# Four graph layers on one core: the normalised adjacency and the masks prepared in layer 0's second step, and the first two aggregations run between layer 0's last products

## The reference

```
x = layernorm(x + L0(x, adj))      # h = x W^T + b, then 8 Euler steps:
                                   #   h += dt * (alpha/2 * (adj h - h) + h w_eff - h + x)
x = layernorm(x + L1(x, adj))      # A = adj + I; deg = row sums + column sums - diagonal
                                   # A_hat = A * deg^-1/2[:, None] * deg^-1/2[None, :]
                                   # agg = A_hat x; h = relu(batchnorm(agg W1^T + b1)); out = batchnorm(h W2^T + b2)
x = layernorm(x + L2(x, adj))      # attention with 4 heads, masked where adj == 0
x = layernorm(x + L3(x, adj))      # graph attention with leaky relu, masked where adj == 0
```

## Time and profile before

| | us |
|---|---|
| median of 3 runs | 969.47 (965.02 to 971.21) |
| span of the profiled execution | 965.1 |
| busy: TensorE, weight load, VectorE, ScalarE, GpSimd | 905.8, 646.9, 641.5, 508.7, 382.7 |

### The profile page before, as it was taken

One profiled execution on the slowest core, in us unless ns is written; L12 is line 12 of the kernel. 1 busy time (PEld: TensorE's weight loads), 2 busy tenths in 40 slices (PEclk: granted clock), 3 DMA queues, 4 the chain that ended last, 5 costly groups with the idle time before them and its releaser, 6 DMA issues. The chain is left out here.

```text
span 965.1 us, 20989 instructions
## 1 busy us (share of the span) xinstructions
PE 905.8 (94%) x6054; PEld 646.9 (67%) x6054; DVE 641.5 (66%) x1944; ACT 508.7 (53%) x919; POOL 382.7 (40%) x433
## 2 busy tenths in 40 slices
PE   6999999999999699977789999999999998999996
PEld 5799999999999688833345544555445453677775
DVE  4754554554554576646466777777777764899997
ACT  4323121121121245555356777777777767788884
POOL 4011121021020130000246777878778777355554
PEclk9999999999999899979889999999999999999999
DMA  8000000000000100000033334333333342011111
GB/s 245 23 12 12 12 23 12 12 22 11 11 11 0 30 15 0 0 1 0 1 79 77 78 71 87 72 79 85 66 81 83 66 87 46 1 33 33 33 33 44
DMA packets 34236, 40.68 MB, mean 42 GB/s; under 512 B 6672, under 2 KB 17552, under 8 KB 34192
## 3 DMA queue, kind: packets, MB, share of 16 engines
q1 hardware_dynamic: 32816, 39.87, 17.3%
q10 hardware_dynamic: 1376, 0.27, 0.1%
HBM read 6.43 MB, written 4.19 MB: 11 GB/s over the span
## 5 line engine op out<-in xcount | busy, mean ns | idle before, releaser
L1754 DVE CUSTOM_DVE_ANT_0 junk<-bank,mask_ij 128x512 bf16<-128x512 f32 x256 | 166.6, 688 | 78.2 <-PE bank L1844 75.6
L1617 POOL TENSOR_TENSOR half_sum<-prob 128x1024 f32<-128x1024 f32 x64 | 151.9, 2381 | 13.6 <-ACT prob L1691 13.6
L1691 ACT ACTIVATE prob<-wide 128x1024 f32<-128x1024 f32 x128 | 125.2, 1017 | 37.2 <-PE wide L1861 32.7
L431 ACT CAST yT<-wide 128x512 fp32r<-128x512 f32 x48 | 28.2, 589 | 206.1 <-PE wide L827 156.8
L531 POOL TENSOR_TENSOR Xr<-Xf,Xr 128x512 fp32r<-128x512 f32 x16 | 20.4, 1292 | 168.1 <-ACT Xr L426 167.9
L1844 PE MATMUL bank<-qkT 32*128 32x512 f32 x256 | 77.1, 504 | 5.2 <-DVE mx L1754 4.3
L1857 PE MATMUL wide<-qk_st 128*128 128x512 f32 x256 | 76.4, 421 | 0.9 <-issue 0.6
L1439 PEld LDWEIGHTS bank<-Wh,pr 128*128 128x128 f32 x512 | 65.3, 191 | 13.5 <-ACT pr L1292 5.3
L59 PE MATMUL bank<-z,L3T_hi 128*128 128x256 f32 x256 | 74.2, 290 | 0.0
L60 PE MATMUL bank<-z,L3T_hi 128*128 128x256 f32 x256 | 73.7, 288 | 0.0
L61 PE MATMUL bank<-z,L3T_lo 128*128 128x256 f32 x256 | 73.7, 288 | 0.0
(11 more groups left out here) (301 smaller groups left out, 2296.1 us busy)
## 6 DMA issues: line engine op xcount, KB each, us to landing
qk_st<-qkT SPq DMA_DIRECT2D x192, 128.0 KB, 2.4
out_dram<-rc SPq DMA_DIRECT2D x15, 256.0 KB, 2.3
Xf<-X SPq DMA_DIRECT2D x14, 256.0 KB, 2.3
A<-in_adj_dram SPq DMA_DIRECT2D x4, 256.0 KB, 4.9
qk_st<-neg_row SPq DMA_DIRECT2D x64, 2.0 KB
Xf<-in_x_dram SPq DMA_DIRECT2D x2, 256.0 KB, 7.0
mask_q<-mask_ji SPq DMA_DIRECT2D x16, 32.0 KB, 1.8
w<-in_L_gnn_W_dram SPq DMA_DIRECT2D x2, 128.0 KB, 2.4
```

The costliest lines, as they stand in the source:

```text
L1617: pool.tensor_tensor(flat(half_sum[h][:]), flat(prob[bp][h][:, 0:2]), flat(prob[bp][h][:, 2:4]), ALU.add).then_inc(h_sum, 1)
L1691: act.activation(flat(prob[bp][h][:, 2 * half:2 * half + 2]), wide[half][:], ACT.Exp, scale=SCALE).then_inc(t_exp, 1)
L1754: dve.tensor_tensor_reduce(out=junk[hh][:], in0=bank[4 + hh][:], in1=m.mask_ij[:, i], scale=1.0, scalar=3.0 * MASKED, op0=ALU.add, op1=ALU ...
```

## The change

`SECOND` takes in the eight turns of A (`#t`, `#A`) with all that goes with them; all of them use one PSUM bank, number 7, one after the other, where `LAST` had used four banks. dinv is made by GpSimd in step 1. `LAST` loses them and takes in aggregations 0 and 1 and hidden product 0. Xa high of batches 0 and 1 is made ahead of the z of step 8, and its low part by GpSimd. SyncE's DMAs move: L2's and L3's weights to the start, the 16 blocks of mask_q ahead of the last weights, w1 and w2 to after the last batch but one. Hb is laid out by batch first. Cut to its core:

```diff
 SECOND = {
-    "PE": ORDER,
-    "ACT": order("h h y z z N y z z y A p p g p g g p g #s0 y z z y z z y p p g g n p p g g a"),
-    "DVE": order("h h y z z N y z z y A p p g #i0 p g g p g y z z y z z y p p g g n p p g g a"),
+    "PE": order("y #t0 y #t1 y p p #t2 g p g #t3 g p g y y y #A0 p p g #A1 g p p #A2 g g #A3"),
+    "ACT": order("h h #s0 y #t0 z z y #t1 z z y #t2 #t3 y z z y z z y #A0 #A1 #A2 #A3"),
+    "DVE": order("y #m0 z z y #m1 z z y p p #m2 g #i0 p g #m3 g p g #G0 y z z #D0 y z z y p p #A0 g g n #A1 p p "
+                 "#A2 g g a #A3"),
 }
 LAST = {
-    "PE": order("#t0 #t1 #t2 #t3 #w0 p p p p #A0 #A1 #A2 #A3 p p p p #v0"),
-    "ACT": order("z z z z #t0 #t1 #t2 #t3 #x0 #x1 z z z z #A0 #A1 #A2 #A3"),
-    "DVE": order("z z N z z A #m0 #m1 p p #m2 #m3 #G0 p p #D0 z z z z #A0 #x0 #x1 #w0 p #A1 p #A2 p #A3 p n #v0 #a0 a"),
+    "PE": order("#w0 #a0 p p p p #a1 #h0 p p p p #v0"),
+    "ACT": order("#x0 #x1 z z z z #a0 z z z z #a1 #h0 #x2"),
+    "DVE": order("N z z z z A p p #a0 p p z z z z #w0 p p p p #x2 #a1 n #W0 #v0 a"),
 }
-LATE = {"PE": ORDER, "ACT": order("#v0"), "DVE": order("N #x2 #a1 A")}
+LATE = {"PE": ORDER, "ACT": order("#v0"), "DVE": order("N A")}
...
-T_BANKS = bank[0:3] + bank[7:8]
+T_BANK = bank[7]
...
# GpSimd
+if isinstance(s, int) and s == groups:
+    for b in range(2):
+        pool.wait_ge(la_x_hi, after(b, 1))
+        pool.tensor_tensor(flat(Xa[b][1][:]), batch_flat(m.X, b), flat(Xa[b][0][:].bitcast(F32)),
+                           ALU.subtract).then_inc(la_x_lo, 1)
...
-if isinstance(s, int) and s == groups:
+if isinstance(s, int) and s == 1:
     pool.wait_ge(v_deg, 2)
...
# TensorE
 elif what == "#t":
-    turn(A, k, T_BANKS[k], t_AT)
+    if k == 0:
+        pe.wait_ge(c_cB, 3)
+    else:
+        pe.wait_ge(c_AT, k)
+        pe.wait_ge(v_mji, k)
+    turn(A, k, T_BANK, t_AT)
...
 elif what == "#A":
-    pe.wait_ge(v_As, 2 * NT)
-    pe.wait_ge(v_mji, k + 1)
-    turn(A, k, T_BANKS[k], t_Ah)
+    if k == 0:
+        pe.wait_ge(v_As, 2 * NT)
+        pe.wait_ge(v_mji, NT)
+    else:
+        pe.wait_ge(c_Ah, k)
+        pe.wait_ge(v_Ah, k)
+    turn(A, k, T_BANK, t_Ah)
```

More of the change, by code:

```diff
@@ L373, in _ @@
                     sp.dma_start(L1.par2[:, k], ins[f"L1_gnn_{n}"].rearrange("(p a) -> p a", a=1)).then_inc(la_par_in, 16)
[L374 to L382, removed]
             sp.wait_ge(la_w_in, 2 * 16)
             sp.wait_ge(la_par_in, 6 * 16)
-            sp.wait_ge(w3_in, 2 * 16)
+            sp.wait_ge(w3_in, 16)
+            sp.wait_ge(a3_in, 16)
             sp.wait_ge(qkv_in, 16)
@@ L486, in step @@
                         act.wait_ge(t_Ah, k + 1)
-                        act.activation(m.AhT[0][:, k], T_BANKS[k][:], ACT.Copy, scale=dinv[:, k:k + 1]).then_inc(c_Ah, 1)
+                        act.activation(m.AhT[0][:, k], T_BANK[:], ACT.Copy, scale=dinv[:, k:k + 1]).then_inc(c_Ah, 1)
             pairs(act, groups, 3, step)
             def aggregate_step(s, par, alive, nth):
[L492 to L511, removed]
+                early = isinstance(s, int) and s < 3
+                if alive[0] and not early:
+                    batch_high(s, par, nth)
+                if alive[1] and not early:
+                    aggregate_high(s - 1, 1 - par)
+                if alive[2] and not early:
+                    hidden_out(s - 2, par)
+            pairs(act, B, 4, aggregate_step)
         @block.gpsimd
@@ L606, in batch_low @@
                 dve.wait_ge(la_x_hi, after(b, 1))
+                dve.wait_ge(la_x_lo, after(b - 1, 1))
                 dve.tensor_tensor(flat(Xa[par][1][:]), batch_flat(m.X, b), flat(Xa[par][0][:].bitcast(F32)),
@@ L910, in step @@
+                        pe.matmul(bank[7][:, 0:2], L1.W3T[:], L1.a3[:], start=True, stop=True).then_inc(wa_ps, 1)
                     elif what == "#A":
-                        pe.wait_ge(v_As, 2 * NT)
-                        pe.wait_ge(v_mji, k + 1)
-                        turn(A, k, T_BANKS[k], t_Ah)
+                        if k == 0:
[4 more added lines that the diff above has]
+                            pe.wait_ge(v_Ah, k)
@@ new lines, in step, with aggregate @@
+                        turn(A, k, T_BANK, t_Ah)
+            def aggregate(b, par):
+                if isinstance(b, int) and b == 0:
+                    pe.wait_ge(v_Ah, NT)
+                pe.wait_ge(la_x_lo, after(b, 1))
+                pe.wait_ge(la_a_lo, after(b - 2, 1))
+                for k in range(NT):
+                    last = three_pass(pe, bank[par][:], [h[:, k] for h in Xa[par]],
+                                      [h[:, k] for h in m.AhT], start=(k == 0), stop=(k == NT - 1))
+                last.then_inc(la_a_ps, 1)
@@ new lines, in hidden @@
+            def hidden(b, par):
+                if isinstance(b, int) and b == 0:
+                    pe.wait_ge(la_w_lo, 1)
+                if isinstance(b, int) and b == 1:
+                    pe.wait_ge(h_sb, after(groups - 1, 2 * NT))
+                pe.wait_ge(la_a_lo, after(b, 1))
+                for c in range(CH):
+                    pe.wait_ge(la_h_sb, after(b - 2, CH, c + 1))
+                    three_pass(pe, bank[2 + 2 * par + c][:], [h[:, c] for h in W1T],
+                               [h[:] for h in agT[par]]).then_inc(la_h_ps, 1)
@@ L915, in _ @@
             pairs(pe, groups, 3, step)
             def aggregate_step(s, par, alive, nth):
-                if alive[1]:
-                    b = s - 1
-                    if isinstance(s, int) and s == 1:
-                        pe.wait_ge(v_Ah, NT)
-                    pe.wait_ge(la_x_lo, after(b, 1))
-                    pe.wait_ge(la_a_lo, after(b - 2, 1))
-                    for k in range(NT):
-                        last = three_pass(pe, bank[1 - par][:], [h[:, k] for h in Xa[1 - par]],
-                                          [h[:, k] for h in m.AhT], start=(k == 0), stop=(k == NT - 1))
-                    last.then_inc(la_a_ps, 1)
@@ L928, in aggregate_step @@
-                if alive[2]:
-                    b = s - 2
-                    if isinstance(s, int) and s == 2:
-                        pe.wait_ge(la_w_lo, 1)
-                        pe.wait_ge(wa_c, 3)
-                        pe.wait_ge(h_sb, after(groups - 1, 2 * NT))
-                    pe.wait_ge(la_a_lo, after(b, 1))
-                    for c in range(CH):
-                        pe.wait_ge(la_h_sb, after(b - 2, CH, c + 1))
-                        three_pass(pe, bank[2 + 2 * par + c][:], [h[:, c] for h in W1T],
-                                   [h[:] for h in agT[par]]).then_inc(la_h_ps, 1)
+                early = isinstance(s, int) and s < 3
@@ L940, in _ @@
+                if alive[1] and not early:
+                    aggregate(s - 1, 1 - par)
+                if alive[2] and not early:
+                    hidden(s - 2, par)
             pairs(pe, B, 4, aggregate_step)
@@ L966, in at @@
             return t
[L968 removed]
+        self.Hb = at("Hb", [P, B, CH, N])
         self.W2T = at("W2T", [P, CH, P])
```

66 lines of the change are left out of this document (50 added, 16 removed).

## The result

| | median of the runs, us | runs | profiled execution, us |
|---|---|---|---|
| before | 969.59 | 965.02 to 971.21 | 965.1 |
| after | 974.75 | 974.02 to 977.37 | 972.8 |

The ratio of after to before is 1.0069, with a 95% interval of 1.0038 to 1.0100: slower by some 0.4 to 1.0%. The medians differ by 5.2 us, the two profiled executions by 7.7; the forecast was +3.6. In the experiments further down, one of the 11 executions of the kernel before that e8 is compared with took 1255.5 us at a mean granted clock of 0.65; it is left out of the ratio.

The account below looks back on a forecast made before the run. TensorE bounds layer 0's loop and the aggregation loop, VectorE's queue the stretch before aggregation 3. 8.7 - 7.7 + 0.5 + 2.1 = +3.6 us: 968.7 profiled, 973 median; range 962 to 981, 80% within about 1%.

Parts of the forecast that it names:

- Eight turns in step 1: Step 1 of layer 0: eight turns of four transposes add 0.44 us each, 3.5 us of TensorE time.
- rival B: Step 1: hand-overs of the one bank not covered, up to 11.9 us on top, median 985; 8%.
- Copies in front of the next step's input: Step 2: scaled copies delay Xr and the root through in-order queues; two TensorE waits, 5.2 us together.
- wait for z: Step 2: TensorE wants VectorE's z pair at 114.7, it ends at 117.6; wait of 2.9 us.
- wait for Xr: Step 2: TensorE waits 2.3 us before y1 for GpSimd's low part of Xr.
- term of 8.7 us: Delay until the last G product: 3.5 of turns plus waits of 2.3 and 2.9 us.
- Rival C: Step 2: the clock also falls at the two waits, 1.7 to 2.5 us each, median 977 to 978; 20%.
- Step 8: Last G product to last product on TensorE: 28.5 us become 20.7, at full clock.
- The tail: VectorE's queue from its last p to #x of batch 3: 12.0 us, so TensorE waits 6.7 us before aggregation 3.
- Rival A: Aggregation 3: TensorE, not VectorE's tail, sets its start, 5.2 us earlier, median 964; 8%.
- The half clock behind the wait: From aggregation 3 on: half speed after the idle stretch costs 1.7 to 2.5 us, taken as 2.1.
- DMAs, the low parts on GpSimd, the layout of Hb: Moved DMAs, low parts on GpSimd, new Hb layout: taken at nothing, each bounded by 0 to 1 us.

Follow-up runs that it names:

- e8: Kernel after with the reorderings of e1 and e2, aggregation 0 ahead of the W1 transposes, weights' and batch 2's splits earlier on VectorE: 961.73 us, 0.9926 of before.
- e2: Kernel after with turns #A1 to #A3 moved up by two to three products in step 1: median 969.5 us, ratio to before 1.0002.
- e1: Kernel after with layer 1's preparation moved ahead of layer 0's end on VectorE and ScalarE, TensorE's order untouched: median 967.26 us, ratio to before 0.9998.
- e6: Kernel after with 24 matmuls of unused result put in front of aggregation 3: 973.1 us in one timed execution.
- e3: Kernel after with the aggregations, hidden product and preparation from batch 2 on put back behind step 8, adjacency still early: 968.71 us, ratio to before 1.0006.
- e9: Kernel after, unchanged, run once more for a second trace: 968.67 us.

## Why the prediction was right

The forecast was +3.6 us and 973; measured are +5.2 in the medians (974.75) and, at the mark, +4.6 and +3.8 in two pairs of traces. The mechanism came out as forecast at both places where the change loses time; one number in the sum was close in part by luck, as said below for the clock. Step by step:

*Eight turns in step 1.* 0.44 us each were taken, 3.5 together; step 1 grew by 3.79, 0.47 each. No wait in step 1, for bank 7 or anything else: rival B did not occur, though the tightest margin had been put at 0.2 us.

*Copies in front of the next step's input.* The chain as forecast was ScalarE's copy to 107.3, Xr high, GpSimd's low parts, the root, then VectorE. ScalarE and GpSimd in the kernel after:

```profile
106.85 0.69 ACT L513 ACTIVATE AhT_hi<-bank,dinv 128x512 fp32r<-128x512 f32 x1 [2.87 <-PE bank L819]
107.43 1.12 ACT L448 CAST Xr<-Xf 128x512 fp32r<-128x512 f32 x2
```

```profile
108.12 2.50 POOL L546 TENSOR_TENSOR Xr<-Xf,Xr 128x512 fp32r<-128x512 f32 x2 [19.25 <-ACT Xr L448]
...
110.99 1.01 POOL L155 TENSOR_TENSOR n_rstd<-n_rstd,neg_half 128x4 f32<-128x4 f32 x1
```

and VectorE, the last of the statistics that the root needs, its apply, its part of #A3 and the z pair that TensorE needs:

```profile
101.40 0.38 DVE L146 BATCH_NORM_AGGREGATE n_aggr<-n_stats 128x2 f32<-128x6 f32 x4
...
112.15 1.12 DVE L181 TENSOR_SCALAR X<-zf,n_aggr,n_rstd 128x128 f32<-128x128 f32 x4 [5.24 <-POOL n_rstd L155]
113.18 0.74 DVE L788 SCALAR_TENSOR_TENSOR AhT_lo<-bank,dinv,AhT_hi 128x512 fp32r<-128x512 f32 x1
...
117.00 0.75 DVE L658 TENSOR_TENSOR z<-G,z 128x256 fp32r<-128x256 f32 x2
```

The wait for Xr was put at 2.3 us and took 2.25. The z pair was put at 117.6 and ended at 117.75. The apply idles 5.24 us for a root whose input was ready at 101.78. GpSimd stood idle for 19.25 us until 108.12, waiting for Xr with the root queued behind the two low parts of Xr; made ahead of them, the root would have been done before 104 by these rows' lengths (an estimate), instead of 112.0. That order on GpSimd was not tried; it would also show how much of the wait for z was the root. e2 removed the whole pattern by changing the order of step 1 alone. The Trainium skill ("TensorE: Matmul & The Clock Gate", table of specifications) has ScalarE's, VectorE's and GpSimd's queues as strictly first in, first out; these rows and e2 agree with that.

The wait for z was put at 2.9 us. It was 2.71 in e1 and e6, and 1.13 in the kernel after: there the clock had already fallen behind the first wait, so TensorE reached the z products late. The last G product ended at 327.15, for a forecast of 326.7. Worked out from the rows, the 9.15 us of delay are 3.79 of turns, 2.25 and 1.13 of waits, and a remainder of 1.98. Nearly all of that is the half clock: counted from each trace's own start of step 1 to the end of the last G product (251.08 us before, 260.14 after, 261.69 in e1, 255.21 in e2), less the growth of step 1 and the waits, the remainder is 1.9 us in the kernel after, 1.8 in e1 and 0.1 in e2, which has no fall there. So the term of 8.7 us was close in part by luck: a fall of the clock that the sum had at nothing took what the second wait had too much.

*Rival C* was half right, and this is the one place where the mechanism was missed. I gave 20% to a clock that falls at both waits of step 2, for up to 8.6 us together. It fell in step 2 behind exactly one of the two in each of the five traces that have both: behind the first in after, its second trace and e3; behind the second in e1 and e6. Behind the first it is nearly free, since it shortens the second wait by 1.6 us and costs 1.9; behind the second it costs in full: the transposes behind the last G product start at 329.71 in e1 and at 327.89 in the kernel after. The forecast should have had one fall. It is worth 0.3 us behind the first wait (1.9 less 1.6) and 1.8 behind the second.

*Step 8.* 20.7 us forecast from the last G product to the last product, 21.0 measured; single waits 0.7, 0.2 and 0.7 forecast, 0.74, none and 0.61 measured. The last product ended at 348.1, forecast 347.4.

*The tail.* 12.0 us forecast from VectorE's p to the end of `#x`, 11.8 measured (348.31 to 360.15). Aggregation 3 was put at 359.6 and started at 360.21, the wait for Xa at 6.7 and was 6.4. That VectorE, not TensorE, sets this start is what e1 shows: with TensorE's list untouched and VectorE's reordered, aggregation 3 started at 355.55 without a wait, although all else ran 1.8 us later. e3 fits: VectorE's tail ended at the same time there, with quite another list on TensorE. Rival A fell with that.

*The half clock behind the wait.* 2.1 us taken; against the 60.3 of before, 2.5 in the first trace, 1.5 in the second and 1.8 in e2.

*Sum at the mark*, first pair of traces: 9.15 until the last G product; step 8 from 28.5 to 21.0, so -7.5; from there to aggregation 3, 12.1 for 11.7, so +0.4; the clock 2.5. That is +4.6, the shift of the mark. The excess over +3.6 is in the first term (0.45), in step 8 (0.2) and in the clock (0.4). The 3.1 us further on in the profiled pair were not forecast, and the other traces show them to be no steady effect of the change.

*DMAs, the low parts on GpSimd, the layout of Hb* were taken at nothing. TensorE's waits hold none of them; none was tried alone.

## What to carry to other kernels

Work pulled forward into a gap of one engine can bring nothing if the next thing that the engine needs stands at the end of another engine's queue: follow that queue to the instruction in question before counting the gain, and move the preparation along with the work. A copy put last in a step stands in front of the next step's input on an in-order engine, and the delay is passed on through each queue behind it (here a copy of 0.7 us, which could start only when the step's last turn was done, led to 3.4 us of waits); three products left to run behind that turn, instead of none, removed this. Compare two kernels at a mark behind the change, in two traces each, before explaining a difference of some us in the total.

## What the runs showed of the hardware

Which of two waits a fall of the clock follows isn't fixed by the kernel. Idle stretches of 2.25 us in step 2 were followed by half clock in three traces (0.63 to 0.68 over the next 4.5 to 5 us) and by full clock in two, with the same order of instructions up to there. An idle 1.96 us was followed by 0.66 in e3; the idle 1.12 us of step 2 by a clock of 1.00. But the length of the last idle stretch doesn't settle it. In layer 2 of the kernel before the clock fell at about 477.9 us, where the longest idle stretch of TensorE since 467.1 was 0.99 us:

```profile
474.91:477.91 3.00, 2.42 (x8) 1.00 0.00 0
477.91:480.91 3.00, 3.00 (x9) 0.52 0.00 0
```

In the first trace of the kernel after it stood at 0.50 from 482 to 494 us with TensorE busy throughout, and in e9, with the same instructions and an idle 0.99 us at the same place, it stayed at 1.00. The same 15 us of layer 2 ran at 0.84 and 0.89 in two executions of the kernel before and at 0.56 and 1.00 in two of the kernel after. The 35 runs of the kernel before on one chip spread from 962.7 to 973.9 us; that the clock accounts for this spread was not shown.

Four fp32 transposes of 128x128 in a stream took 0.47 us of TensorE time (3.79 us for eight turns); twelve in a row had taken 0.44 per four.
